# A two-layer graph network step: weight turns behind the first tiles, the takes spread over eight tiles, seven counting columns a pair, projection weights behind h1

## Chip, cores and metric

The kernel runs on one core of one Trainium2 chip. The metric is the device time in microseconds (us), given as the median of the runs. "Tile" below is 512 rows of the node table.

## What is computed

The input is a table x of 50,000 rows by 256 in float32 and 75,000 edges (src, dst), sorted by dst. They include a self edge for every node. Two layers follow each other, each with a residual:

```
h = relu(layernorm(x));  x = x + L0(h, src, dst)
h = relu(layernorm(x));  x = x + L1(h, src, dst)

L0: h = h @ w1.T + b1
    h = relu((h - mean) * rsqrt(var + eps) * gamma + beta)   # mean, var over all nodes
    xw = (h @ w2.T + b2) @ w_gcn.T
    deg = segment_sum(ones, dst) with one self loop more per node;  dinv = rsqrt(deg)
    out = segment_sum(xw[src] * dinv[src] * dinv[dst], dst) + b_gcn
L1: q, k, v = h @ Wq + bq, h @ Wk + bk, h @ Wv + bv          # 8 heads of 32
    a = softmax over the edges with the same src of (q[src] . k[dst])
    out = segment_sum(a * v[dst], src) @ Wo + bo
```

## The kernel before, in words

The node table has 98 tiles. All five engines run programs of their own and meet at semaphores. The kernel is a row of parts that end one after another; the change touches the first two.

**Part A, the first pass** (to about 605 us). For every tile SP loads x (two buffers, a_x), DVE takes the row moments (L215, L219), ACT the standard deviation (L648), DVE reciprocal and shift (L226, L228), and ACT normalises into a_hn (L652). PE turns a_hn (L680, eight transposes), ACT copies the turn to a_ht (L642), PE multiplies by w1 (L702) into one PSUM tile a_h_ps, ACT adds the bias and copies to h1 (L634) and stores it (L627), and DVE takes the column statistics of h1 (L1024). An engine's program is a list of steps; in step s it works on tile s less a lag: PE turns tile s - 1 and multiplies tile s - 3, ACT copies the turn of tile s - 2 and h1 of tile s - 4, DVE counts h1 of tile s - 5. `over_pairs` writes PE's and DVE's steps out, but for the pairs of tiles inside a hardware loop; `over_tiles` does the same for SP and ACT with one loop. A tile on PE waits until ACT has copied the last product out of a_h_ps.

Ahead of its first step PE waits for all seven loads of weights, turns w1 and w_gcn into turn_ps (L731), mixes w2 with w_gcn (L736) and the bias b2 with w_gcn (L739). ACT copies the results (L614, L616, L617), then issues eight loads of w_out (L621), and only then takes its first step.

Beside its tiles DVE sorts the edges for later parts (`beside_tile`, once per tile outside the loops). Tile 1 has the first preparation of the edge words (`pack_words`), tile 3 the second (`close_words`) and then all takes (`take_all`). A *take* finds the 8 largest of 294 words in each half of every partition, copies them to `found` and strikes them out (L836, L840, L841). The number of takes depends on the data; `take_all` is a loop over it. The class work, `decode_words` and what follows, stands behind tiles `class_tile` = 4 to 15. From pair `hist_pair` = 8 on DVE makes one-hot rows (L758, L759) of `hist_most` = 6 columns of edges a pair, three behind each tile. PE adds them up in hist_ps (L672), and POOL scatters the same columns to a table (L591). 240 columns make 40 pairs. These pairs are the loop `hist_loop`.

**Part B, the second pass** (to about 1145 us). SP loads h1 back (L1149), ACT applies the batch norm (L1198), PE multiplies by w_mix (L1231), DVE adds b_mix (L1310), ACT scales and stores y and agg_out. Between its tiles DVE and PE sort the takes by source. At its start SP loads two tiles of h1, waits for the turned roots of the degrees, stores them, loads the slots (L1169), then the projection weights and biases of the second layer (seven DMAs, L1171 to L1173), and only then h1 of tile 2. DVE searches the largest exponent of these weights (`find_peak`, L1323) behind its fourth tile step.

## Time and profile before

| | |
|---|---|
| median of 3 runs | 3427.66 us (3424.08 to 3429.75) |
| the profiled execution's own time | 3436.49 us |
| its span | 3434.7 us |
| mean granted TensorE clock in it | 0.967 |
| busy, share of the span | PE 90%, PE weight loads 73%, DVE 82%, ACT 73%, POOL 57% |
| DMA | 861 MB moved, mean 251 GB/s |

The profile is of one execution. The slices divide the span in 40 equal parts of 85.9 us and give each engine's busy share in tenths. In the timeline a row is one instruction or several alike merged: start and duration in us, engine, line, operation, output and inputs, count, and in brackets how long the engine had been idle before and what ended that. PEld is the load of a stationary operand; float32 matmuls show as two records each. SPq and ACTq rows are the issuing of DMAs. Busy shares of windows are sums over records in that stretch. The granted clock is the share of 2.4 GHz that TensorE was given.

### The profile page before, as it was taken

The numbers are of one execution on the slowest core, as the hardware profiler recorded it, in microseconds if no ns is written. First come the engines' busy times: TensorE is split into PE (matmuls) and PEld (weight loads), VectorE is DVE, ScalarE is ACT, GpSimd is POOL, SyncE is SP. The second block draws the span as 40 slices with busy tenths as digits, with TensorE's granted clock in tenths as the row PEclk, the third lists the DMA queues.
The fourth block names the chain that finished last, engine by engine and source line by source line (L and its number), as shares of the span: only waits on it lengthen the run. The fifth ranks groups of instructions, "written<-read, shape, count | busy, mean of one in ns | idle before, by whom it ended". The sixth has DMA issues, their size and how long they took to land. (4 is left out here: it accounts for less than half of the span.)

```text
span 3434.7 us, 80752 instructions
## 1 busy us (share of the span) xinstructions
PE 3104.5 (90%) x20244; PEld 2498.7 (73%) x20244; DVE 2809.3 (82%) x7375; ACT 2502.0 (73%) x7074; POOL 1953.0 (57%) x1668
## 2 busy tenths in 40 slices
PE   2899999799998489999999999994999999999999
PEld 1455554577775278787888878883899999999998
DVE  6888887787886478888888888884888888888887
ACT  2688888699896567676777777762777777777776
POOL 1055554155554377777777777763555555555553
PEclk6899999999999699999999999996999999999999
DMA  2455555688886578888878888865677777777774
GB/s 76 147 204 203 203 202 182 233 300 309 301 306 234 206 271 297 305 296 293 304 293 303 296 305 293 302 257 182 230 249 258 258 254 250 254 254 257 254 248 157
DMA packets 335634, 861.27 MB, mean 251 GB/s; under 512 B 98484, under 2 KB 152923, under 8 KB 323019
## 3 DMA queue, kind: packets, MB, share of 16 engines
q1 hardware_dynamic: 238794, 677.69, 55.3%
q0 software_dynamic: 66256, 78.94, 7.7%
q10 hardware_dynamic: 30512, 103.83, 7.6%
q8 instruction: 27, 0.44, 0.1%
q14 instruction: 45, 0.36, 0.0%
HBM read 521.95 MB, written 416.52 MB: 273 GB/s over the span
## 5 line engine op out<-in xcount | busy, mean ns | idle before, releaser
L1848 PE MATMUL c_qkv_ps<-w_qkv_hi,c_ht_hi 128*128 128x256 f16 x2352 | 642.3, 273 | 0.0
L1848 PE MATMUL c_qkv_ps<-w_qkv_lo,c_ht_hi 128*128 128x256 f16 x2352 | 642.3, 273 | 0.0
L1848 PE MATMUL c_qkv_ps<-w_qkv_hi,c_ht_lo 128*128 128x256 f16 x2352 | 642.3, 273 | 0.0
L2281 ACT ACTIVATE e_mine<-e_mine,e_attention 128x32 f32<-128x32 f32 x2352 | 518.7, 308 | 42.3 <-issue 26.1
L2228 POOL DMA_INDIRECT e_kv<-kv_table,e_near x392 | 401.5, 1024 | 113.4 <-issue 102.7
L1718 POOL DMA_INDIRECT c_got<-y_table,c_near x392 | 395.1, 1008 | 108.7 <-issue 87.9
L591 POOL DMA_INDIRECT dst_slots<-dst_word,dst_goal x240 | 241.3, 1005 | 304.3 <-ACT a_hn L652 235.9
L2317 PE MATMUL e_out_ps<-w_out,e_mean_t 128*128 128x256 f32 x1568 | 392.8, 380 | 0.0
L2220 POOL TENSOR_TENSOR e_kv<-e_kv,e_part_of 128x1024 f32<-128x1024 f32 x98 | 187.0, 1908 | 350.8 <-DVE e_part_of L2550 350.8
L702 PE MATMUL a_h_ps<-a_ht,w_t 128*128 128x512 f32 x784 | 368.9, 614 | 17.8 <-ACT h L634 13.9
L1482 POOL DMA_INDIRECT src_slots<-staged_word,staged_goal x240 | 235.2, 980 | 254.5 <-DVE sort_lane_hot L1371 119.2
L1231 PE MATMUL mix_ps<-w_mix,hb 128*128 128x256 f32 x1568 | 358.0, 382 | 12.7 <-ACT hb L1198 9.8
L1231 PEld LDWEIGHTS mix_ps<-w_mix,hb 128*128 128x128 f32 x1568 | 297.2, 191 | 59.0 <-ACT hb L1198 12.6
L1711 POOL TENSOR_TENSOR c_x<-c_agg,c_x 128x1024 f32<-128x1024 f32 x98 | 231.4, 2361 | 161.3 <-ACT c_agg L1765 151.9
L2317 PEld LDWEIGHTS e_out_ps<-w_out,e_mean_t 128*128 128x128 f32 x1568 | 267.4, 191 | 44.0
L1835 PE MATMUL c_sum_ps<-c_got,c_sum_hot 128*128 128x256 f32 x784 | 217.2, 400 | 87.3 <-DVE c_agg L1957 58.5
L702 PEld LDWEIGHTS a_h_ps<-a_ht,w_t 128*128 128x128 f32 x784 | 144.8, 195 | 184.2 <-issue 184.1
L1776 ACT ACTIVATE c_hn<-c_x,c_shift,c_rstd 128x256 f32<-128x256 f32 x392 | 203.5, 590 | 95.7 <-DVE c_shift L1978 94.8
L1703 POOL TENSOR_TENSOR c_qk<-c_q,c_kv 128x1024 f32<-128x1024 f32 x98 | 232.0, 2367 | 34.9 <-DVE c_kv L1942 32.6
L1848 PEld LDWEIGHTS c_qkv_ps<-w_qkv_lo,c_ht_hi 128*128 128x128 f16 x2352 | 230.5, 98 | 27.1
L1848 PEld LDWEIGHTS c_qkv_ps<-w_qkv_hi,c_ht_lo 128*128 128x128 f16 x2352 | 230.5, 98 | 27.1
L2273 ACT ACTIVATE e_mean_t<-e_mean_ps 128x512 f32<-128x512 f32 x196 | 114.9, 586 | 184.9 <-PE e_mean_ps L2331 163.8
(433 smaller groups left out, 7781.8 us busy)
## 6 DMA issues: line engine op xcount, KB each, us to landing
kv_table<-c_kv SPq DMA_DIRECT2D x98, 1024.0 KB
h_table<-h ACTq DMA_DIRECT2D x98, 512.0 KB
h<-h_table SPq DMA_DIRECT2D x98, 512.0 KB
y_table<-y_out ACTq DMA_DIRECT2D x98, 512.0 KB
agg_table<-agg_out SPq DMA_DIRECT2D x98, 512.0 KB
c_agg<-agg_table SPq DMA_DIRECT2D x98, 512.0 KB
x_table<-c_x SPq DMA_DIRECT2D x98, 512.0 KB
q_table<-c_q SPq DMA_DIRECT2D x98, 512.0 KB
```

The costliest lines, as they stand in the source:

```text
L591: nc.gpsimd.indirect_dma_start(out=dst_slots, out_offset=bass.IndirectOffsetOnAxis(ap=dst_goal[:, k:k + 1], axis=0), in_=dst_word[:, k:k + ...
L702: last = nc.tensor.matmul(h1_ps[:, oc * TILE:(oc + 1) * TILE], w1_t[:, kc, oc * P:(oc + 1) * P], ht[u][:, kc, :], start=kc == 0, stop=kc = ...
L1231: last = nc.tensor.matmul(mix_ps[u][:, j * D:(j + 1) * D], hb[u][:, kc, j * P:(j + 1) * P], w_mix[:, kc, :], start=kc == 0, stop=kc == KC - 1)
L1482: nc.gpsimd.indirect_dma_start(out=src_slots, out_offset=bass.IndirectOffsetOnAxis(ap=staged_goal[h][:, k:k + 1], axis=0), in_=staged_word ...
L1703: nc.gpsimd.tensor_tensor(qk[u][:, :, :], qb[w][:, :, :], kv[w][:, :, 0, :], ALU.mult).then_inc(qk_ready, 1)
L1711: nc.gpsimd.tensor_tensor(x1[u][:, :, :], agg[w][:, :, :], xb[w][:, :, :], ALU.add).then_inc(x1_ready, 1)
L1718: nc.gpsimd.indirect_dma_start(out=got[w][:, j, :], out_offset=None, in_=y_table, in_offset=bass.IndirectOffsetOnAxis(ap=near[w][:, j:j + ...
L1835: last = nc.tensor.matmul(sum_ps[:, j * D:(j + 1) * D], sum_hot[w][:, row, :], got[w][:, row, :], start=True, stop=True)
L1848: last = nc.tensor.matmul(qkv_ps[n][:, j * D:(j + 1) * D], h[u][:, kc, j * P:(j + 1) * P], wt[:, kc, n * D:(n + 1) * D], start=m == 0, sto ...
L2228: nc.gpsimd.indirect_dma_start(out=kv[w][:, j, :], out_offset=None, in_=kv_table, in_offset=bass.IndirectOffsetOnAxis(ap=near[w][:, j:j + ...
L2281: last = nc.scalar.activation(of_head, of_head, ACT.Copy, scale=attention[u][:, j, h, 0:1])
L2317: last = nc.tensor.matmul(out_ps[:, j, :], mean_t[u][:, kc, row * P:(row + 1) * P], w_out[:, kc, :], start=False, stop=kc == KC - 1)
```

## The change

Four things are changed.

1. PE's and ACT's first steps stand ahead of the weights. PE turns w1 and w_gcn behind its transposes of tile 1 (into a_h_ps instead of turn_ps), mixes w2 behind those of tile 2 and b2 behind those of tile 4 (both into hist_ps). ACT copies the turned weights behind tile 1, the mixed ones behind tiles 4 and 5. The eight loads of w_out are issued by SP, behind the edges. The class sums in hist_ps wait for the last copy.
2. Two takes stand behind each of tiles 4 to 11 (`take_pair` = 2, `take_pairs` = 4; pairs 3 to 5 are a loop, `take_loop`). The data-dependent rest, at least one take, is a loop behind tile 12 (`take_rest`). `class_tile` is 12, so all class work comes eight tiles later.
3. `hist_pair` becomes 12, so the columns have fewer pairs: `hist_most` is 7, four columns in the first tile of a pair and three in the second, and the loop has 34 pairs. The scatters on POOL go with them.
4. In part B the seven loads of projection weights stand behind the load of h1 tile 5, and `find_peak` stands behind DVE's sixth tile step.

```diff
-        self.takes_beside = -(-self.wide // TAKEN)
-        self.most_extra = max(1, self.most_takes - self.takes_beside + 1)
-        self.class_tile = 4
+        self.take_pair = 2
+        self.take_pairs = 4
+        self.takes_beside = 4 * self.take_pairs
+        self.most_extra = max(1, self.most_takes - self.takes_beside)
+        self.class_tile = 2 * (self.take_pair + self.take_pairs)
...
+                take_loop = (3, plan.take_pair + plan.take_pairs)
...
-                    return k is not None or i - plan.hist_pair in hist_pairs
+                    return k == 1 or (k is None and i - plan.hist_pair in hist_pairs)
...
+                            rows_of_head = wo.rearrange("(d h) n -> h d n", h=H)
+                            for h in range(H):
+                                kc, first = divmod(h * DH, P)
+                                sp.dma_start(w_out[first:first + DH, kc, :], rows_of_head[h]).then_inc(out_loaded, 16)
...
+                    sp.wait_ge(out_loaded, 16 * H)
...
+                    def copy_weights():
+                        for b, w in enumerate((w1_t, wg_t)):
+                            act.wait_ge(weights_turned, b + 1)
+                            nc.scalar.activation(w[:, :, :].rearrange("p a b -> p (a b)"), h1_ps[:, b * TILE:(b + 1) * TILE], ACT.Copy).then_inc(weights_copied, 1)
+
+                    def copy_mix():
+                        act.wait_ge(mixed, 1)
+                        nc.scalar.activation(w_mix[:, :, :].rearrange("p a b -> p (a b)"), hist_ps[:, 0:TILE], ACT.Copy).then_inc(weights_copied, 1)
+
+                    def copy_mix_bias():
+                        act.wait_ge(mixed, 2)
+                        nc.scalar.activation(b_mix[:, :], hist_ps[:, 0:D], ACT.Copy).then_inc(weights_copied, 1)
 
...
+                            if isinstance(i, int) and i * 2 + u == 1:
+                                copy_weights()
+                            if isinstance(i, int) and i * 2 + u == 4:
+                                copy_mix()
+                            if isinstance(i, int) and i * 2 + u == 5:
+                                copy_mix_bias()
...
-                    act.wait_ge(out_loaded, 16 * H)
...
+                        if s == 2:
+                            turn_weights()
+                        if s == 3:
+                            mix_weights()
+                        if s == 5:
+                            mix_bias()
                         if s == plan.class_tile + 6:
+                            pe.wait_ge(weights_copied, 4)
...
+                    def turn_weights():
+                        pe.wait_ge(weights_loaded, 16 * 7)
+                        for b, w in enumerate((w1_n, wg_n)):
+                            for kc in range(KC):
+                                for oc in range(KC):
+                                    at = b * TILE + kc * D + oc * P
+                                    last = nc.tensor.transpose(h1_ps[:, at:at + P], w[:, oc, kc * P:(kc + 1) * P], ident[:, :])
+                            last.then_inc(weights_turned, 1)
+                        pe.wait_ge(weights_copied, 2)
+
+                    def mix_weights():
+                        for kc in range(KC):
+                            for jc in range(KC):
+                                last = nc.tensor.matmul(hist_ps[:, kc * D:(kc + 1) * D], w2_n[:, jc, kc * P:(kc + 1) * P],
+                                                        wg_t[:, jc, :], start=jc == 0, stop=jc == KC - 1)
+                        last.then_inc(mixed, 1)
+
+                    def mix_bias():
+                        pe.wait_ge(weights_copied, 3)
+                        for jc in range(KC):
+                            last = nc.tensor.matmul(hist_ps[:, 0:D], b2_c[:, jc:jc + 1].to_broadcast([P, P]), wg_t[:, jc, :],
+                                                    start=jc == 0, stop=jc == KC - 1)
+                        last.then_inc(mixed, 1)
+
                     pe.wait_ge(const_ready, const_of_ident)
...
-                    over_pairs(pe, plan, 3, step, (hist_loop,))
+                    over_pairs(pe, plan, 3, step, (take_loop, hist_loop))
...
-                        link(v.tensor_scalar(rounds_f[:, 3:4], rounds_f[:, 2:3], -float(plan.takes_beside - 1), 1.0, ALU.add, ALU.max))
+                        link(v.tensor_scalar(rounds_f[:, 3:4], rounds_f[:, 2:3], -float(plan.takes_beside), 1.0, ALU.add, ALU.max))
...
-                    def take_all():
+                    def take_rest():
                         dve.wait_ge(const_ready, const_all)
                         more = dve.value_load(rounds[0:1, 3:4], min_val=0, max_val=plan.most_extra - 1) + 1
-                        with dve.Fori(0, more + (plan.takes_beside - 1)) as n:
-                            take(n)
-                        hold(dve, replaced, more * 2 + (2 * plan.takes_beside))
+                        with dve.Fori(0, more) as n:
+                            take(n + plan.takes_beside)
+                        hold(dve, replaced, more * 2 + (2 * plan.takes_beside + 2))
...
-                            take_all()
+                        elif 0 <= tile - 2 * plan.take_pair < 2 * plan.take_pairs:
+                            for m in two:
+                                take(2 * (tile - 2 * plan.take_pair) + m)
                         elif at == 0:
+                            take_rest()
...
-                            if k is None:
+                            if k == 0:
+                                for m in two:
+                                    take(i * 4 + (u * 2 + m - 4 * plan.take_pair))
+                            elif k is None:
...
+                    def load_qkv():
+                        for i, (w, b) in enumerate(((wq, bq), (wk, bk), (wv, bv))):
+                            sp.dma_start(w_qkv[:, :, i * D:(i + 1) * D], w.rearrange("(c p) n -> p c n", p=P)).then_inc(qkv_loaded, 16)
+                            sp.dma_start(b_raw[:, i * D:(i + 1) * D], b.partition_broadcast(P)).then_inc(qkv_loaded, 16)
+                        sp.dma_start(b_out_n[:, :], bo.partition_broadcast(P)).then_inc(qkv_loaded, 16)
...
+                            if isinstance(i, int) and i * 2 + u == 5:
+                                load_qkv()
...
-                            if isinstance(b, int) and b == 0 and t == 3:
+                            if isinstance(b, int) and b == 0 and t == 5:
```

The left-out lines take the old forms away: the weight turns ahead of PE's steps, the copies and w_out loads ahead of ACT's, and the projection loads behind `slots` in part B.

How the instructions move, in program order. On DVE, from the end of `close_words` (the last row of the second preparation, `rounds`) before: the takes are one loop, and tile 4's moments come behind it.

```order
L840 ISA
L840 COPY found<-edge_best 128x8
L841 MATCH_REPLACE words<-edge_best,words 128x294
L840 ISA
L840 COPY found<-edge_best 128x8
L841 MATCH_REPLACE words<-edge_best,words 128x294
L846 ISA
L846 COMPARE_AND_BRANCH
L341 ISA
L215 BN_STATS a_stats<-a_x 128x6 x4
L219 BN_AGGR a_moments<-a_stats 128x2 x4
```

The same place on DVE in the change (its own line numbers), from the last row of `close_words` on:

```order
L856 CAST rounds<-rounds_f 128x4
L217 BN_STATS a_stats<-a_x 128x6 x4
L221 BN_AGGR a_moments<-a_stats 128x2 x4
L228 RECIPROCAL a_rstd<-a_std 128x4
L230 SCALAR_TENSOR_TENSOR a_shift<-a_moments,a_rstd 128x4
L866 MAX edge_best<-words 128x8 x2
L870 COPY found<-edge_best 128x8
L871 MATCH_REPLACE words<-edge_best,words 128x294
L870 COPY found<-edge_best 128x8
L871 MATCH_REPLACE words<-edge_best,words 128x294
L866 MAX edge_best<-words 128x8 x2
```

Tile 4's moments and shift now follow the preparation directly, and its two takes stand behind them, ahead of tile 5.

On ACT, before, from the last bias load on (w_t and wg_t are the turned weights, w_mix and b_mix the mixed ones):

```order
L610 DMA b_c<-in_L_gnn_b 128x2x1
L614 ACT_TABLE_LOAD
L614 ACTIVATE w_t<-a_turn_ps 128x512
L614 ACTIVATE wg_t<-a_turn_ps 128x512
L616 ACTIVATE w_mix<-a_turn_ps 128x512
L617 ACTIVATE b_mix<-a_turn_ps 128x256
L621 DMA w_out<-in_L_gnn_Wo 32x256 x8
L648 ACT_TABLE_LOAD
L648 ACTIVATE a_std<-a_moments,eps_col 128x4
L652 ACTIVATE a_hn<-a_x,a_shift,a_rstd 128x256 x4
L648 ACTIVATE a_std<-a_moments,eps_col 128x4
L652 ACTIVATE a_hn<-a_x,a_shift,a_rstd 128x256 x4
```

and in the change:

```order
L618 DMA b_c<-in_L_gnn_b 128x2x1
L659 ACT_TABLE_LOAD
L659 ACTIVATE a_std<-a_moments,eps_col 128x4
L663 ACTIVATE a_hn<-a_x,a_shift,a_rstd 128x256 x4
L659 ACTIVATE a_std<-a_moments,eps_col 128x4
L663 ACTIVATE a_hn<-a_x,a_shift,a_rstd 128x256 x4
L624 ACTIVATE w_t<-a_h_ps 128x512
L624 ACTIVATE wg_t<-a_h_ps 128x512
L653 ACTIVATE a_ht<-a_turn_ps 128x512 x2
L659 ACTIVATE a_std<-a_moments,eps_col 128x4
L663 ACTIVATE a_hn<-a_x,a_shift,a_rstd 128x256 x4
```

Tiles 0 and 1 are normalised ahead of the copies of the turned weights, one table load is gone, and no w_out load is left on ACT.

On SP at the start of part B, before, from the load of `slots` on:

```order
L1169 DMA slots<-dst_slots 128x392
L1171 DMA w_qkv<-in_L_gnn_Wq 128x2x256
L1172 DMA b_raw<-in_L_gnn_bq 128x256
L1171 DMA w_qkv<-in_L_gnn_Wk 128x2x256
L1172 DMA b_raw<-in_L_gnn_bk 128x256
L1171 DMA w_qkv<-in_L_gnn_Wv 128x2x256
L1172 DMA b_raw<-in_L_gnn_bv 128x256
L1173 DMA b_out_n<-in_L_gnn_bo 128x256
L1149 DMA h_0<-h_table 128x1024
L1149 DMA h_1<-h_table 128x1024
L1149 DMA h_0<-h_table 128x1024
```

and in the change:

```order
L1213 DMA slots<-dst_slots 128x392
L1191 DMA h_0<-h_table 128x1024
L1191 DMA h_1<-h_table 128x1024
L1191 DMA h_0<-h_table 128x1024
L1205 DMA agg_table<-agg_out 128x1024
L1191 DMA h_1<-h_table 128x1024
L1186 DMA w_qkv<-in_L_gnn_Wq 128x2x256
L1187 DMA b_raw<-in_L_gnn_bq 128x256
```

The h1 loads of tiles 2 to 5 and the first store of agg_out now stand ahead of the weights, and the store of agg_out of tile 1 behind them.

## Rows read from the trace of the kernel before

**Rows 1.** The page's 40 slices, PE's busy tenths.
```profile
PE   2899999799998489999999999994999999999999
```

**Rows 2.** Timeline, part A's start: start, duration, engine, line, what, idle before.
```profile
6.15 0.38 DVE L219 BATCH_NORM_AGGREGATE a_moments<-a_stats 128x2 f32<-128x6 f32 x4
...
11.61 1.11 PE L731 MATMUL a_turn_ps<-ident,w_n 128*128 128x128 f32 x4 [11.61 <-DMA b_c<-in_L_gnn_b]
...
24.43 1.28 ACT L648 ACT_TABLE_LOAD   x1 [2.88 <-issue]
...
26.06 0.18 DVE L226 RECIPROCAL a_rstd<-a_std 128x4 f32<-128x4 f32 x1 [19.53 <-ACT a_std L648]
```

**Rows 3.** Timeline, DVE: preparations of the words, two takes, tile 4.
```profile
29.06 0.77 DVE L782 CAST edges_f<-edges 128x1176 f32<-128x1176 int32 x1
...
42.15 0.46 DVE L801 TENSOR_SCALAR work_i<-work_i 128x588 int32<-128x588 int32 x1
...
51.42 0.83 DVE L836 MAX8 edge_best<-words 128x8 f32<-128x294 f32 x2 [1.39 <-issue]
...
53.17 0.82 DVE L836 MAX8 edge_best<-words 128x8 f32<-128x294 f32 x2
...
77.88 1.41 DVE L215 BATCH_NORM_STATS2 a_stats<-a_x 128x6 f32<-128x256 f32 x4 [0.22 <-DVE words L841]
```

**Rows 4.** Timeline, PE and its weight loads behind the takes.
```profile
82.60 1.97 PE L680 MATMUL a_turn_ps<-ident,a_hn 128*128 128x128 f32 x8 [30.48 <-ACT a_hn L652]
...
85.22 0.34 PEld L702 LDWEIGHTS a_h_ps<-a_ht,w_t 128*128 128x128 f32 x1 [0.52 <-issue]
...
86.07 0.34 PEld L702 LDWEIGHTS a_h_ps<-a_ht,w_t 128*128 128x128 f32 x1 [0.52 <-issue]
```

**Rows 5.** Timeline of the column loop, then its window (PE, PEld, DVE, ACT, POOL busy).
```profile
302.38 0.66 PE L672 MATMUL hist_ps<-hot_hi,hot_lo 128*128 128x392 f16 x3
...
303.95 0.32 DVE L758 TENSOR_SCALAR hot_hi<-lane,dst_key 128x392 f16<-128x392 f16 x1
...
303.99 3.67 PE L702 MATMUL a_h_ps<-a_ht,w_t 128*128 128x512 f32 x8
...
304.34 0.32 DVE L758 TENSOR_SCALAR hot_hi<-lane,dst_key 128x392 f16<-128x392 f16 x1
...
309.24 3.67 PE L702 MATMUL a_h_ps<-a_ht,w_t 128*128 128x512 f32 x8 [0.21 <-ACT h L634]
...
314.36 3.67 PE L702 MATMUL a_h_ps<-a_ht,w_t 128*128 128x512 f32 x8
...
300.00:400.00 100.00, 97.30 (x365) 51.27 (x364) 88.28 (x346) 86.68 (x174) 58.59 (x59) 1.00 0.57 200
```

**Rows 6.** Timeline, DVE, tile 8: its moments and the h1 statistics in it.
```profile
108.90 1.41 DVE L215 BATCH_NORM_STATS2 a_stats<-a_x 128x6 f32<-128x256 f32 x4
...
111.38 1.28 DVE L1024 BATCH_NORM_STATS2 bn_stats<-h 128x6 f32<-128x512 f32 x2
```

**Rows 7.** Timeline, DVE: the starts of tiles 5, 16 and 24.
```profile
83.53 1.40 DVE L215 BATCH_NORM_STATS2 a_stats<-a_x 128x6 f32<-128x256 f32 x4
...
161.84 1.41 DVE L215 BATCH_NORM_STATS2 a_stats<-a_x 128x6 f32<-128x256 f32 x4 [0.21 <-DVE uneven_cols L940]
...
203.00 1.39 DVE L215 BATCH_NORM_STATS2 a_stats<-a_x 128x6 f32<-128x256 f32 x4
```

**Rows 8.** Window of tile 7: busy, then granted clock, DMA share, GB/s.
```profile
105.40:113.60 8.20, 4.76 (x16) 2.29 (x16) 7.70 (x26) 4.49 (x10) 0.00 (x0) 0.94 0.40 145
```

**Rows 9.** Timeline, part B's start (SP's queue and PE), then a window behind it.
```profile
623.43 9.41 SPq L1149 DMA_DIRECT2D h<-h_table  x3
...
624.79 3.62 PE L1231 MATMUL mix_ps<-w_mix,hb 128*128 128x256 f32 x16
...
632.54 3.72 PE L1231 MATMUL mix_ps<-w_mix,hb 128*128 128x256 f32 x16 [2.39 <-ACT hb L1198]
...
640.00:644.00 4.00, 2.86 (x16) 1.78 (x15) 3.83 (x18) 3.70 (x9) 0.00 (x0) 1.00 0.95 360
```

More of the change, by code:

```diff
@@ L733, in _ @@
-                    pe.wait_ge(weights_copied, 2)
-                    for kc in range(KC):
-                        for jc in range(KC):
-                            nc.tensor.matmul(turn_ps[1][:, kc * D:(kc + 1) * D], w2_n[:, jc, kc * P:(kc + 1) * P],
-                                             wg_t[:, jc, :], start=jc == 0, stop=jc == KC - 1)
-                    for jc in range(KC):
-                        last = nc.tensor.matmul(turn_ps[1][:, TILE:TILE + D], b2_c[:, jc:jc + 1].to_broadcast([P, P]), wg_t[:, jc, :],
-                                                start=jc == 0, stop=jc == KC - 1)
```

25 lines of the change are left out of this document (1 added, 24 removed).

## The prediction

> **What bounds the kernel now.** I read the slices of the page first, since they show where the matrix engine (PE) is not full. In the part that the change touches most, layer one's first pass (the first 605 of 3435 us), PE is full except in the first slice [rows 1]. Then I read the timeline there, engine by engine. The vector engine (DVE) has tile 0's moments at 6.5 us and then stands still for 19.53 us: the standard deviation that comes next waits on ACT behind the weight copies, eight DMA issues and a second table load, and the copies wait for weights that land at 11.6 [rows 2]. Later it is the other way round: DVE runs the takes alone, from 51.4 to 77.7, and PE is idle for 30.48 us [rows 3, 4]. In the steady stretch a pair of tiles takes 314.36 - 303.99 = 10.37 us, with PE 97%, DVE 88% and ACT 87% busy [rows 5]: nearly a balance, in which PE's products and the h1 copy on ACT set the pace. So what is saved before tile 24 is still saved at the end of the pass, if that balance holds. The chain that ended last lies in a later part and does not help here.
>
> **Step 1, the first tiles go ahead of the weights.** Tile 0's moments are ready at 6.5. ACT then needs its one table load, 1.28 us [rows 2]; standard deviation, reciprocal and shift follow, so tile 1 begins on DVE at about 8.6 and the first preparation of the edge words at about 11.5. From that preparation to the second it is 42.15 - 29.06 = 13.1 us, two tiles' moments among them [rows 3]. The second then starts at 11.5 + 13.1 = 24.6 instead of 42.15: **17.5 us** gained. The weight turns fit in between, since PE gets to them at about 14, after 11.6. The edges were issued ahead of the weights' last column and should be there at 11.5; if they land 2 us late, everything moves by 2. The eight w_out DMAs cost ACT 2.88 us of issue ahead of its table load [rows 2]; on SP they stand between the edges and tile 2's load, which waits until tile 0 is normalised at about 10.7 anyway. Without that cover they would cost 2.9.
>
> **Step 2, the takes.** A take is 53.17 - 51.42 = 1.75 us, and fifteen of them with their entry fill 50.0 to 77.9 [rows 3]. That block goes. The second preparation lasts 50.0 - 42.15 = 7.9, so tile 4 begins at 32.5, and tiles 4 to 11 carry two takes each. A tile without extra work costs DVE 111.38 - 108.90 + 1.28 = 3.76 us [rows 6], so a take tile is 3.76 + 3.49 = 7.25; eight are 58.0, less 1.3 because tile 4 has no h1 statistics. The cover for PE here is DVE: a tile's PE work is 8 x 0.85 + 1.97 = 8.8 us at the lower clock [rows 4], and at the higher a whole tile takes 5.1 to 5.3 [rows 5]. I add 1.5 for tile 4, where the first product, behind the mixing of the weights, may keep ACT from its standard deviation (0 to 3.4, half a product at the lower clock), and 1.5 for entering and leaving the new loop. No row shows such an entry alone; the nearest is the 1.39, with a register load, ahead of the takes [rows 3], so 0 to 3. Tile 12 begins at 32.5 + 58.0 - 1.3 + 3.0 = 92.2.
>
> **Step 3, the rest of the takes.** Sixteen are done by then and one more always runs, so there are two more than before. Tile 12 is old tile 4 (83.53 - 77.88 = 5.65 [rows 3, 7]) plus 1.3 of h1 statistics plus 1.39 + 1.75 + 0.2 for the last take: 10.3, to 102.5. Tiles 13 to 23 do what 5 to 15 did, 161.84 - 83.53 = 78.3 us, so tile 24 begins at 180.8. In the trace it begins at 203.0 [rows 7]. Steps 1 to 3 give **22.2 us**: 17.5 from the start and only 4.7 from the takes, because a take tile is 2 us longer than a steady one and two takes are added.
>
> **Step 4, seven columns a pair.** The 240 columns move from 40 pairs to 34. A tile's fourth column costs DVE 0.39 and PE at most 0.66 / 3 = 0.22 [rows 5]. The totals do not change; what counts is the slack in that tile. PE waits 0.21 for the h1 copy in one tile of each pair and not visibly in the other. So the price lies between 0 and 34 x 0.22 = 7.5 us. I take 1, since the tile without a visible wait still cannot start its product before the copy it needs. POOL goes from 58.6% busy [rows 5] to about 68%, and nobody waits for it before the pass ends.
>
> **Step 5, the projection weights.** At the start of the second pass SP issues 7 DMAs (1.28 MB) and only then, at 623.43, h1 tile 2; PE ends tile 1's product at 628.4 and starts tile 2's at 632.54 [rows 9]. With h1 first, the tile is there before PE wants it, and with its sort columns in between PE starts at about 629.4: 3.1 gained. The loads now fall behind tile 5's, where the 16 DMA engines are 0.95 busy [rows 9]; 1.28 MB at the 360 GB/s of that row is 3.6 us, half of which I count as given back by later tiles. The peak search that waits for them moves two tiles down with them. Net **1.3 us**, between a loss of 2 and a gain of 4.
>
> The Trainium skill (DMA: Bandwidth & Descriptors, on issuing engines) says that DMAs started by the scalar, sync or gpsimd engine all run on the same 16 engines and interleave. By that rule w_out saves no transfer time on SP and the projection loads only change place: step 5 would be 0 and the sum 1.3 less. No row here separates the two.
>
> **Sum.** 22.2 - 1.0 + 1.3 = 22.5 us. Against the profiled execution's own 3436.5 that is 3414.0. It stands 8.8 above the median of the three timed runs, 3427.7, and the saving is the same there: **3405.2**.
>
> **Rivals.**
> *The clock stays low in the take tiles.* For it: PE comes out of idle at the lower level, where a tile costs 8.8 us [rows 4]. Against it: from 105.4 to 113.6, with PE busy 4.8 of 8.2 us, the granted clock was 0.94 [rows 8]. At 1.2 GHz in all eight tiles PE would set 8.8 instead of 7.25: 12.4 lost, gain 10, 3417.6. The Trainium skill (TensorE: Matmul & The Clock Gate, Part 1) says that the throttled state is the default and activity releases it; by that rule 8.8 us of work in 7.25 could not stay throttled, and this rival would fall away. The trace agrees in that one window.
> *The balance breaks in the column pairs.* DVE's 0.39 and PE's 0.22 both land on the path: 0.61 x 34 = 21, gain 2.6, 3425. For it: 97% and 88% busy. Against it: both engines have some slack per pair, and all other tiles keep three columns.
> *Slower: the takes are not covered at all.* If something in the pipeline (the single h1 bank, or the h1 statistics that ACT waits for) makes a tile's matrix work and its takes run one after another, a take tile costs 8.8 + 3.5 = 12.3 us. Eight are 98.4, 40.4 more than I count: 22.5 becomes a loss of 17.9, 3445.6. It decides from a take tile of 7.25 + 22.5 / 8 = 10.1 us. Against it: DVE issues the shift and the h1 statistics ahead of the takes, so PE and ACT hold all that they need.
> *Nothing gained at the start:* something that I do not see, such as late edges, holds tile 0 or 1 back; the takes' 4.7 remain, 3422.7.
>
> **How the numbers follow.** My forecast with its inner bounds (tile 4, loop entry, columns, loads) has 0.82 and spans 3396 to 3415. The low clock has 0.07, the broken balance 0.03, nothing at the start 0.05, the slower case 0.03. The range is **3396 to 3416**: the forecast and a part-time low clock, about 0.15 left out. About 0.2% (6.9 us) is what a measurement of this kernel tells from no change. Faster by more: the forecast, the low clock and part of the others, 0.93; within: 0.04; slower: 0.03.
>
> **What would show it.** DVE: first reciprocal at about 8.3 and no idle of 19 us; second preparation at 24 to 26; take tiles 7.1 to 7.6 apart; tile 12's moments near 92 and tile 24's near 181. PE: no empty stretch of 30 us; pairs of 10.4 to 10.5 in the column loop. Second pass: tile 2's product within 1.5 us of tile 1's end. Wrong would be: take tiles above 8, pairs of 10.9, edges landing past 14 us, or a later product of the second pass held by h1's DMA for more than 3 us.

## The result, and the profile after

The changed kernel takes 3450.6 us (median of 20 runs) against 3427.6: a ratio of 1.0061, 95% interval 1.0039 to 1.0083. It is slower by 0.6%. The forecast was 22.5 us less, 3405.2 us, with a range of 3396 to 3416. Its runs scatter from 3422.1 to 3474.5 us, those of the kernel before only from 3424.1 to 3432.5. The profiled execution took 3447.9 us, near its median; that of the kernel before lay 8.8 us above its own.

The page of the changed kernel: the 40 slices, PE's busy tenths and its granted clock.

```profile
PE   6788998799998489999999999994999999999999
...
PEclk9999999899999779999999999996999999999999
```

The first slice went from 2 to 6 [rows 1], but slices 3, 4 and 7 fell from nine to eight and slice 2 from eight to seven. The start, in the timeline of the changed kernel:

```profile
5.87 0.38 DVE L221 BATCH_NORM_AGGREGATE a_moments<-a_stats 128x2 f32<-128x6 f32 x4
...
6.32 1.28 ACT L659 ACT_TABLE_LOAD   x1 [6.32 <-DVE a_moments L221]
...
7.95 0.18 DVE L228 RECIPROCAL a_rstd<-a_std 128x4 f32<-128x4 f32 x1 [1.70 <-ACT a_std L659]
...
10.95 0.77 DVE L812 CAST edges_f<-edges 128x1176 f32<-128x1176 int32 x1
...
24.08 0.46 DVE L831 TENSOR_SCALAR work_i<-work_i 128x588 int32<-128x588 int32 x1
...
32.23 1.40 DVE L217 BATCH_NORM_STATS2 a_stats<-a_x 128x6 f32<-128x256 f32 x4 [0.25 <-DVE rounds L856]
...
38.20 1.39 DVE L217 BATCH_NORM_STATS2 a_stats<-a_x 128x6 f32<-128x256 f32 x4
...
90.71 1.39 DVE L217 BATCH_NORM_STATS2 a_stats<-a_x 128x6 f32<-128x256 f32 x4
...
99.52 1.41 DVE L217 BATCH_NORM_STATS2 a_stats<-a_x 128x6 f32<-128x256 f32 x4
...
176.52 1.41 DVE L217 BATCH_NORM_STATS2 a_stats<-a_x 128x6 f32<-128x256 f32 x4 [0.22 <-DVE uneven_cols L970]
```

DVE's idle time of 19.53 us [rows 2] is 1.70. Tiles 4, 5, 12, 13 and 24 begin in the last five rows; tile 24 stood at 203.00 [rows 7], so 26.5 us are gained where the column loop begins, more than the 22.2 of the forecast. At the start of the second pass all of it is gone. Its first products after the change, timeline of PE:

```profile
647.04 3.62 PE L1271 MATMUL mix_ps<-w_mix,hb 128*128 128x256 f32 x16
...
652.24 3.62 PE L1271 MATMUL mix_ps<-w_mix,hb 128*128 128x256 f32 x16
```

Tile 1's product stood at 624.79 [rows 9] and is at 647.04: 22.2 us later. So the column loop lost 26.5 + 22.2 = 48.7 us. Two windows of the changed kernel, the one of [rows 8] and the one of [rows 5] (busy of PE, PEld, DVE, ACT, POOL, then granted clock, DMA share, GB/s):

```profile
105.40:113.60 8.20, 5.37 (x8) 2.01 (x8) 7.66 (x25) 2.92 (x7) 0.00 (x0) 0.79 0.27 98
300.00:400.00 100.00, 87.57 (x326) 46.27 (x325) 79.61 (x315) 74.50 (x150) 57.13 (x59) 0.97 0.52 174
```

In the first window, tile 13's and behind the rest of the takes, the granted clock is now 0.79 instead of 0.94. In the loop, the second window, PE fell from 97.3 to 87.6, DVE from 88.3 to 79.6 and ACT from 86.7 to 74.5 [rows 5]: no engine is the bound any more. What they wait for shows in one of six such places, timeline of the changed kernel:

```profile
236.24 3.67 PE L725 MATMUL a_h_ps<-a_ht,w_t 128*128 128x512 f32 x8
...
239.22 0.97 POOL L599 DMA_INDIRECT dst_slots<-dst_word,dst_goal  x1 [1.02 <-DMA dst_slots<-dst_word,dst_goal]
...
240.69 0.97 POOL L599 DMA_INDIRECT dst_slots<-dst_word,dst_goal  x1 [0.49 <-issue]
241.97 1.08 POOL L599 DMA_INDIRECT dst_slots<-dst_word,dst_goal  x1 [0.31 <-issue]
243.35 0.97 POOL L599 DMA_INDIRECT dst_slots<-dst_word,dst_goal  x1 [0.30 <-issue]
244.63 0.97 POOL L599 DMA_INDIRECT dst_slots<-dst_word,dst_goal  x1 [0.30 <-issue]
245.91 0.97 POOL L599 DMA_INDIRECT dst_slots<-dst_word,dst_goal  x1 [0.30 <-issue]
246.64 1.27 ACT L645 ACTIVATE h<-a_h_ps,bn_in 128x512 f32<-128x512 f32 x2 [6.72 <-remote]
...
248.05 4.57 PE L725 MATMUL a_h_ps<-a_ht,w_t 128*128 128x512 f32 x5 [6.77 <-ACT h L645]
```

PE's product ends at 239.91 by its record. The h1 copy on ACT starts at 246.64, and PE then waits for the copy. The copy waits for three semaphores: the product's, that of the store which frees its buffer (its last update stands in the trace at 235.53) and that of the statistics that DVE takes from the buffer (that instruction ended at 239.25). So the product's came last. "Remote" is what the view says when it finds no instruction of the core that ended just before the release; here the release is the product's own semaphore update, which the trace has at 246.48, 6.6 us after the last matmul. In the kernel before 111 of PE's 137 updates that its trace has from 200 to 480 us stand within 0.1 us of theirs. PE went on to the next transposes, which end at 241.28, and DVE to its one-hot rows, until 242.8; from then on only POOL works. The Trainium skill (Perfetto Trace Analysis, Per-engine timelines, on the Tensor Engine's instruction) says that the end of a matmul is the profiler's estimate. No run here can show whether the product was written late or only its semaphore passed on late; this text calls both a late update. The groups of waits from 200 to 600 us, changed kernel (engine, line, waited for: us in total, times, longest):

```profile
POOL dst_slots L599 <- issue: 74.6, 194, 2.8
POOL dst_slots L599 <- ACT a_hn L663: 71.6, 22, 10.2
...
ACT h L645 <- remote: 29.1, 6, 6.9
```

The kernel before has no wait of the kind "remote" in this stretch. It is not free of late updates, though. The other 26 of the 137, one in nearly every pair, come 1.3 to 2.9 us after the transposes, beside the row of six scatters, and no instruction in the profile has to wait for them: the delay is there, but covered.

The 29.1 us of waits are not the whole loss. Behind a stall PE works at the lower clock: the granted clock was 1.00 from 236 to 240 us and 0.50 from 248 to 252. From 203 to 605 us it was 1.00 before and is 0.96 after the change. As an estimate, 0.04 of these 402 us is at most 16 us; with the waits that is up to 45 of the 48.7.

### The profile page after: what moved, and what is told of

Its sections match the earlier page's. It is cut to its first block and busy times, and to the rows that moved or that the text cites. A ratio compares the mean times of both kernels' runs of the same rounds, so it can differ in the third digit from the quotient of the medians.

```text
span 3446.1 us, 80626 instructions
## 1 busy us (share of the span) xinstructions
PE 3119.8 (91%) x20244; PEld 2506.0 (73%) x20244; DVE 2814.0 (82%) x7391; ACT 2504.3 (73%) x7073; POOL 1953.3 (57%) x1668
## 5 line engine op out<-in xcount | busy, mean ns | idle before, releaser
L725 PE MATMUL a_h_ps<-a_ht,w_t 128*128 128x512 f32 x784 | 379.4, 629 | 51.3 <-ACT h L645 43.3
L1888 PEld LDWEIGHTS c_qkv_ps<-w_qkv_hi,c_ht_hi 128*128 128x128 f16 x2352 | 230.5, 98 | 24.7
```

The costliest lines, as they stand in the source:

```text
L725: last = nc.tensor.matmul(h1_ps[:, oc * TILE:(oc + 1) * TILE], w1_t[:, kc, oc * P:(oc + 1) * P], ht[u][:, kc, :], start=kc == 0, stop=kc = ...
L1888: last = nc.tensor.matmul(qkv_ps[n][:, j * D:(j + 1) * D], h[u][:, kc, j * P:(j + 1) * P], wt[:, kc, n * D:(n + 1) * D], start=m == 0, sto ...
```

## The experiments

The theories: **seven a pair** (the column loop loses by the seventh column or its scatter), against **early start** (it loses because it is entered earlier, or through two loops). Once that was settled, the theories became narrower.

One remark on the runs: step 5 alone and the first runs of the rows of twelve, of the even pauses and of six, six, seven ran beside a kernel before that took 3388 us, not 3427, and are compared with that alone. By the record these four, and no others, ran on chip 13; all other runs of this section ran on the chips 7, 11 and 12, where the kernel before took 3426 to 3427 us. For the runs of the result it names no chip.

### Seven columns alone, the early start alone

```
-        self.hist_most = -(-self.wide // (self.tiles // 2 - 1 - self.hist_pair))
+        self.hist_most = 7
```

> The kernel before with seven counting columns and seven scatters a pair (four beside one tile, three beside the next) and nothing else of the change; start and takes as before. Theory 'seven a pair' (the stalls of some 7 us in the column loop come with the seventh column or its scatter): the same stalls appear here, tile distances of 10 to 12 us at five or six places and a colder TensorE behind them; the column loop of the change lost some 47 us between tiles 24 and 97, so 3427.6 + 30 to 50 = 3458 to 3478 us, and the times scatter by tens of us. Rival 'early start' (the loop loses time because it is entered earlier, in another phase against the DMAs, or through two loops): nothing here, 3424 to 3432 us, tile distances of 5.12 and 5.26 us.

Measured: 3498.2 us (3477.2 to 3511.1), ratio 1.0222 [1.02, 1.0244]. Its waits from 180 to 570 us:

```profile
ACT h L634 <- remote: 33.0, 9, 5.2
```

The same stalls, with the start and the takes of the kernel before: 71.5 us lost against the 3426.7 beside it, more than the 30 to 50 that were expected. The other kernel is the changed one with these undone, and the projection weights' place too:

```
-        self.take_pair = 2
-        self.take_pairs = 4
-        self.takes_beside = 4 * self.take_pairs
-        self.most_extra = max(1, self.most_takes - self.takes_beside)
-        self.class_tile = 2 * (self.take_pair + self.take_pairs)
+        self.takes_beside = -(-self.wide // TAKEN)
+        self.most_extra = max(1, self.most_takes - self.takes_beside + 1)
+        self.class_tile = 4
...
                         elif at == 0:
-                            take_rest()
+                            take_all()
...
```

> The kernel before with the early start alone: weight turns behind the first tiles, output weights on SyncE's queue; the block of 26 us of takes at tile 4, six columns a pair and the projection weights as before. Theory 'seven a pair': no stalls, the start's 17.5 to 20 us stay until the end, 3407 to 3410 us, times within some 8 us of each other. Rival 'early start': stalls of 7 us in the loop again, 3430 to 3460 us and scattered.

Measured: 3406.7 us (3405.3 to 3408.7), ratio 0.9947 [0.9933, 0.996], so 20 us less than the 3426.7 beside it (14 to 23 by the interval), and no "remote" wait in the loop. The early start is innocent and gives what step 1 said, within the noise of this measurement.

### Column or scatter?

```
-        self.hist_most = -(-self.wide // (self.tiles // 2 - 1 - self.hist_pair))
-        self.hist_full = self.wide // self.hist_most
+        self.hist_most = 6
+        self.hist_full = 216 // self.hist_most
...
-                    for k in range(WIDTH):
-                        pair, c = divmod(k, per_pair)
+                    for k in range(216):
+                        pair, c = divmod(k, 6)
...
```

> The changed kernel with six columns and six scatters a pair, three a tile. It has 36 pairs for them, so the last 24 of 240 columns are neither counted nor scattered (10 per cent of the one-hots, of the counting products and of the scatters are left out). Theory 'seven a pair': no stalls, tile distances 5.12 and 5.26 us, first tile of the loop at 176 us as in the change, so some 26 us under the kernel before: 3399 to 3404 us, hardly scattered. Rival 'early start': as the change, 3430 to 3460 us, scattered.

Measured: 3407.2 us (3403.8 to 3409.5), 0.9948 [0.9934, 0.9961]. Only the second half of that edit, the loop of scatters, so that PE and DVE keep seven columns:

> The changed kernel with its seven columns a pair for VectorE and TensorE, but GpSimd scatters only six a pair, three beside each tile; the last 24 scatters are left out. If the fourth scatter in a tile (four times 1.28 us are the whole tile of 5.12 us) makes the stalls: none are left, and only the seventh column's own work remains, 3399 to 3410 us. If the four one-hot pairs and counting products in one tile make them: as the change, 3430 to 3470 us, scattered, with TensorE's product ending 7 us late at some places.

Measured: 3401.7 us (3398.7 to 3406.1), 0.993 [0.9917, 0.9944]. A window of it, to be held against the one above:

```profile
300.00:400.00 100.00, 97.87 (x375) 52.19 (x375) 92.37 (x370) 86.39 (x174) 57.01 (x58) 1.00 0.58 204
```

PE is back at 97.9%, and DVE at 92.4 carries the seventh column without a loss. (24 of 240 scatters are left out here; the last experiment below leaves none out and comes to 3407.3 us.) The converse, six columns with seven scatters (the first half of the edit, the loop of scatters left as it is):

> The changed kernel with seven scatters a pair (all 240), but six columns a pair for VectorE and TensorE; 216 of 240 columns are counted, the last 24 are left out. Theory 'scatters alone': the stalls are all there, 3430 to 3470 us, scattered. Rival 'both together' (the fourth scatter stalls TensorE only beside a fourth counting product): few or none, 3402 to 3412 us.

Measured: 3464.6 us (3439.4 to 3481.2), 1.0101 [1.007, 1.0132], with these waits:

```profile
ACT h L645 <- remote: 33.0, 7, 6.8
```

So the scatters alone make the stalls, and the columns' own work costs nothing that shows.

### How the scatters lie in time

```
-            ahead = 3
+            ahead = 2
```

> The changed kernel, seven columns and seven scatters a pair, but each scatter waits for the one two before it to land instead of the one three before it. Theory 'too many in flight' (the stalls need three scatters outstanding while the fourth is issued): with a landing some 2.0 to 2.2 us after the issue, two in flight still allow one scatter in 1.1 to 1.3 us, and no stall is left, 3400 to 3408 us. Rival 'row of scatters' (what counts is that they come one behind the other for a whole tile, 1.28 us apart): as the change, 3430 to 3470 us, scattered.

Measured: 3465.4 us (3463.1 to 3471.7), 1.0117 [1.0102, 1.0132]. By its time this is the rival's result, but the profile says otherwise: there is no "remote" wait, part A's last product is where it is without stalls, and the scatters go on until 642 us, 64 us after it. Timeline, POOL:

```profile
303.27 0.97 POOL L599 DMA_INDIRECT dst_slots<-dst_word,dst_goal  x1 [1.98 <-ACT a_hn L663]
304.55 0.99 POOL L599 DMA_INDIRECT dst_slots<-dst_word,dst_goal  x1 [0.30 <-issue]
307.75 0.97 POOL L599 DMA_INDIRECT dst_slots<-dst_word,dst_goal  x1 [2.21 <-DMA dst_slots<-dst_word,dst_goal]
```

POOL waits after every second or third scatter for a landing. With two in flight the stalls are gone, and a tail takes their place. No update of PE in the trace is more than 0.4 us late here, although seven scatters a pair were asked for: a pause of some 2 us after every two or three is enough.

```
-                    for k in range(WIDTH):
-                        pair, c = divmod(k, per_pair)
+                    for k in range(216):
+                        pair, c = divmod(k, 6)
...
-                        if c == per_tile:
-                            pool.wait_ge(hn_ready[1], pair + 1)
...
```

> The changed kernel with seven columns for VectorE and TensorE, and six scatters a pair as in the run with six scatters, but all six in a row beside the first tile of a pair and none beside the second; the last 24 scatters are left out. Theory 'length of a row' (four and more in a row make the stall): six in a row, 7.7 us of 10.4, stall at least as often as the change, 3430 to 3500 us. Rival 'rate' (seven scatters in 10.38 us are too many, six are not, however they lie): no stalls, 3399 to 3406 us.

Measured: 3408.7 us (3402.7 to 3410.6), 0.995 [0.9937, 0.9963]. It tells nothing new, since my picture of three beside each tile was wrong: the next pair's first wait, `hn_ready[0] >= pair`, asks for a tile that was normalised before the one this pair's second wait asks for. So POOL really stops once a pair: in the kernel before and in the run with six scatters six follow each other, in the change seven.

> The changed kernel with scatters that wait for no tile: from the first on they go one behind the other, three in flight, 1.28 us apart, so all 240 are done 307 us after the first instead of 380 to 410. Theory 'length of a row' or 'rate': stalls again and again while they run, the loop loses at least as much as in the change until some 480 us, nothing after: 3440 to 3520 us. Rival 'phase' (a stall needs a scatter that starts at one moment of the tile, which the wait for the normalised tile fixes): another number of stalls, possibly none, 3400 to 3425 us.

```
-                        if c == 0:
+                        if k == 0:
                             pool.wait_ge(hn_ready[0], pair)
-                        if c == per_tile:
-                            pool.wait_ge(hn_ready[1], pair + 1)
```

Measured: 3672.0 us (3670.1 to 3690.5), 1.073 [1.0709, 1.0751], far worse than any theory had it. Its windows (busy of PE, PEld, DVE, ACT, POOL, clock, DMA share, GB/s) and its longest waits from 230 to 500 us:

```profile
400.00:450.00 50.00, 2.09 (x13) 1.23 (x11) 1.67 (x9) 0.00 (x0) 37.44 (x40) 0.56 0.06 11
...
550.00:600.00 50.00, 48.92 (x185) 25.93 (x184) 45.74 (x183) 43.44 (x89) 0.00 (x0) 1.00 0.55 200
```

```profile
ACT h L643 <- remote: 155.0, 4, 51.2
PE a_h_ps L723 <- issue: 136.0, 3, 49.4
```

While POOL issues a scatter every 1.28 us, PE does 2 us of work in 50; a tile takes some 50 us. When the scatters are done (at 495 us) the loop runs as it should. The DMA engines are 6% busy meanwhile and move 11 GB/s, so this is no contention for transfers. From 200 to 480 us no update of DVE or ACT in this trace comes more than 0.02 us late; PE's are the ones that come late.

### Rate or length of a row?

> The changed kernel with scatters in rows of twelve: one wait every second pair, twelve in a row (15.4 us), then 5.4 us without any, so six in 10.38 us on average; the last 24 scatters are left out. It stands in for the earlier run with six at once, whose rows of six turned out to be those of the kernel before (its waits, too, let six follow each other). Theory 'length of a row' (seven in a row stall, six do not): stalls in each row, 3440 to 3520 us. Rival 'rate' (seven in 10.38 us are too many on average, six are not): none, 3399 to 3409 us.

```
-                        pair, c = divmod(k, per_pair)
-                        pair += plan.hist_pair
+                        pair, c = divmod(k, 12)
+                        pair = plan.hist_pair + 2 * pair
                         if c == 0:
-                            pool.wait_ge(hn_ready[0], pair)
-                        if c == per_tile:
                             pool.wait_ge(hn_ready[1], pair + 1)
...
```

Measured: 3364.8 us, 0.9929 [0.9916, 0.9943], beside 3388.

```
             ahead = 3
+            pause = sb("pause", [P, 170], where=part)
+            paused = sem("paused")
...
+                        if k > 0:
+                            if k > 1:
+                                pool.wait_ge(paused, k - 1)
+                            pool.memset(pause[:, :], 0.0).then_inc(paused, 1)
```

(and the tiles' waits left out, as in the free scatters)

> The changed kernel with all 240 scatters, none of which waits for a tile, but a fill of 170 numbers on GpSimd ahead of each, so that they come one by one some 1.45 to 1.6 us apart, as many in a pair of tiles as in the change, but evenly. Theory 'rate' (seven in 10.38 us): stalls as in the change or worse, 3430 to 3500 us. Rival 'row without a pause' (what holds TensorE's semaphores is that GpSimd goes from one scatter to the next without a pause): no stalls, 3400 to 3410 us, against 3672 us without the fills.

Measured: 3364.2 us, 0.9926 [0.9912, 0.9939], beside 3388; most scatters came 1.4 us apart.

```
-                    for k in range(WIDTH):
-                        pair, c = divmod(k, per_pair)
-                        pair += plan.hist_pair
+                    turn_of_column = [(pair, c) for pair in range(11, NT // 2) for c in range(7 if pair % 3 == 0 else 6)][:WIDTH]
...
+                    for k, (pair, c) in enumerate(turn_of_column):
...
```

> The changed kernel, nothing left out: VectorE and TensorE with seven columns a pair as in the change, scatters from tile 22 on in rows of six, six and seven over the 38 pairs that are left. Theory 'rate' with a threshold near seven, or 'length of a row' with stalls of which each costs some 7 us: at 6.3 in 10.38 us on average the rate theory has none (3400 to 3406 us); the row theory has some at its twelve rows of seven, at a third of the change's frequency (some 3415 to 3425 us, scattered).

Measured: 3364.2 us, 0.9927 [0.9914, 0.9941], beside 3388.

Three patterns and no stall in any. The even pauses alone would have spoken against the rate and the rows of twelve alone against the row, so neither theory fits all three; what fits is that nothing stalls on this chip. So the change itself and the free scatters ran again, beside two of the three.

> The change itself, nothing left out, as a control. Theory 'pattern of the scatters': its stalls are there on any chip, 0.3 to 1.3 per cent above the kernel before, scattered by tens of us. Rival 'another chip': no stalls, 0.7 per cent below the kernel before, as the last runs.

Measured: 3459.9 us (3441.0 to 3471.6), 1.0101 [1.0076, 1.0126], beside 3426.3.

> The scatters spread evenly by a fill of 170 numbers ahead of each, as before. If the pattern counts: 0.6 to 0.8 per cent below the kernel before beside a change that stalls. If rate alone counts and the last chip had no stalls: as slow as the change, 0.3 to 1.3 per cent above.

Measured: 3550.6 us (3531.6 to 3582.0), 1.0383 [1.0352, 1.0415]. Pauses of 0.4 us between all of them are worse than the change's rows of seven. Most scatters came 1.4 us apart and all 240 took 354 us, 1.48 us each, so some seven in 10.38 us, no more than in the change. At the same rate, pauses that are even but short cost more than rows with a longer one behind them.

> Rows of six, six and seven from tile 22 on, as before. Rate theory with a threshold above 6.3 in 10.38 us: 0.6 to 0.8 per cent below the kernel before, beside a change that stalls. Row theory: a third of the change's stalls, 0 to 0.4 per cent below, scattered.

Measured: 3442.0 us (3424.2 to 3456.6), 1.0041 [1.0019, 1.0064]. Timeline, the row of seven that began at 293.08 ends here, and a row of six follows:

```profile
299.57 1.01 POOL L599 DMA_INDIRECT dst_slots<-dst_word,dst_goal  x1 [0.30 <-issue]
300.89 0.97 POOL L599 DMA_INDIRECT dst_slots<-dst_word,dst_goal  x1 [0.30 <-issue]
303.46 0.97 POOL L599 DMA_INDIRECT dst_slots<-dst_word,dst_goal  x1 [1.60 <-ACT a_hn L663]
...
310.22 1.04 POOL L599 DMA_INDIRECT dst_slots<-dst_word,dst_goal  x1 [0.40 <-DMA dst_slots<-dst_word,dst_goal]
312.14 1.26 ACT L645 ACTIVATE h<-a_h_ps,bn_in 128x512 f32<-128x512 f32 x2 [3.70 <-remote]
313.55 5.37 PE L725 MATMUL a_h_ps<-a_ht,w_t 128*128 128x512 f32 x8 [3.43 <-ACT h L645]
```

Behind a row of seven the pause is 1.60 us, behind a row of six 2.67. This execution has 7 "remote" waits (23.0 us) in 180 to 570 us, where a row of seven comes every third pair. No such wait was found in a kernel with rows of six alone, though all five of them whose traces were taken on these chips have the covered late updates of the kernel before.

> The scatters that wait for no tile and have no pauses, as before: some 7 per cent above the kernel before if the stalls are a matter of the pattern on any chip; at most 1 per cent above if the first chip alone had them.

Measured: 3676.3 us (3671.7 to 3678.2), 1.073 [1.0715, 1.0746]: the first result again.

> Rows of twelve scatters (15.4 us), then 5.4 us without any, as before; the last 24 scatters are left out. In the runs on one chip each row of seven of the pattern six, six, seven came with one stall of some 7 us behind it and no row of six did. Row theory: stalls at all eighteen rows, 5 to 14 us each, 2 to 7 per cent above the kernel before. Rate theory: none, 0.6 to 0.8 per cent below. Should the kernel before take some 3388 us beside it, as it did once, it tells nothing.

Measured: 3556.9 us (3547.4 to 3564.2), 1.0378 [1.0363, 1.0393], beside 3427.4. Its waits, 180 to 570 us, then one row of twelve in the timeline, begun at 361.92:

```profile
ACT h L643 <- remote: 82.9, 11, 7.8
```

```profile
361.92 0.97 POOL L597 DMA_INDIRECT dst_slots<-dst_word,dst_goal  x1 [14.15 <-ACT a_hn L661]
...
362.88 3.67 PE L723 MATMUL a_h_ps<-a_ht,w_t 128*128 128x512 f32 x8 [0.21 <-ACT h L643]
...
366.58 1.26 ACT L643 ACTIVATE h<-a_h_ps,bn_in 128x512 f32<-128x512 f32 x2 [0.18 <-PE a_h_ps L723]
...
368.00 3.67 PE L723 MATMUL a_h_ps<-a_ht,w_t 128*128 128x512 f32 x8
...
376.62 0.97 POOL L597 DMA_INDIRECT dst_slots<-dst_word,dst_goal  x1 [0.30 <-issue]
379.35 1.26 ACT L643 ACTIVATE h<-a_h_ps,bn_in 128x512 f32<-128x512 f32 x2 [7.81 <-remote]
380.75 3.75 PE L723 MATMUL a_h_ps<-a_ht,w_t 128*128 128x512 f32 x4 [7.71 <-ACT h L643]
```

The average rate was meant to be that of the kernel before, six in 10.38 us; with the stalls the rows of twelve come some 30 us apart, so it is four. And it stalls at row after row. The product that ended at 366.55, 4.6 us into the row, reached ACT at once; the one that ended at 371.67, 9.8 us into it, reached ACT at 379.35, after the last scatter of the row. So what counts is how long the scatters go on without a real pause, not their rate. The rate theory falls. How long the pause must be was not found: 0.4 us was too short, some 2 us after two or three scatters and 2.7 us after six were enough.

### Step 5 alone, and a kernel that leaves nothing out

```
                                 load_h1(i, u)
+                            if isinstance(i, int) and i * 2 + u == 5:
+                                load_qkv()
...
-                            if isinstance(b, int) and b == 0 and t == 3:
+                            if isinstance(b, int) and b == 0 and t == 5:
                                 find_peak()
```

> The kernel before with the projection weights loaded behind h1 of tile 5 and nothing else of the change. Prediction step 5: 1.3 us less, bounds 4 us less to 2 us more, so 3425 us against 3426.5, nothing that the measurement can tell. Rival 'it frees the whole start of part B' (all that stood between TensorE's first and second product of part B was this load): 4 to 8 us less, 3419 to 3423 us.

Measured: 3390.5 us against 3388.3, 1.0006 [0.9996, 1.0015], 11 runs: 1.4 us less to 5 more. The rival's 4 to 8 us are not there. Step 5's 1.3 us less lies at the edge of the interval: it is not shown, and not quite excluded.

> The changed kernel, nothing left out: seven columns for VectorE and TensorE, scatters in rows of six from tile 22 on, the last twelve without a pause behind those of the last pair. Row theory: no stall in the loop; the last row of fifteen begins with the last tile and ends some 19 us later, with the landing 21 us, against 20 us until part A is done in the run with six scatters: 3402 to 3412 us, the upper end if the row holds TensorE's last products. Rate theory: the same, nearer to 3402.

```
                     for k in range(WIDTH):
-                        pair, c = divmod(k, per_pair)
-                        pair += plan.hist_pair
-                        if c == 0:
+                        pair, c = divmod(k, 6)
+                        pair += plan.hist_pair - 1
+                        if c == 0 and pair < NT // 2:
                             pool.wait_ge(hn_ready[0], pair)
-                        if c == per_tile:
+                        if c == 3 and pair < NT // 2:
                             pool.wait_ge(hn_ready[1], pair + 1)
```

Measured: 3407.3 us (3404.5 to 3412.8), 0.9946 [0.9933, 0.996], faster than both kernels, with nothing left out: 43 us less than the change's 3450.6. The last scatters, timeline of POOL and SP:

```profile
582.54 0.97 POOL L599 DMA_INDIRECT dst_slots<-dst_word,dst_goal  x1 [0.31 <-issue]
587.03 0.81 SPq L1191 DMA_DIRECT2D h<-h_table  x2
```

In the run with six scatters the second pass loaded h at 582.74 us, here at 587.03: 4 us of the takes' gain go into the tail. So it ends where the early start alone ends (3406.7), and of the two that one is the simpler.

## Why the prediction was wrong, step by step

**Step 1 was right.** First reciprocal 7.95 (8.3 forecast), first preparation 10.95 (11.5), second 24.08 (24.6). That is 18.1 us ahead, 17.5 forecast, and alone it gave 20 us (14 to 23 by the interval).

**Step 2 was right.** Tiles 5 to 11 took (90.71 - 38.20) / 7 = 7.50 us each, 7.25 forecast. Tile 4 took 5.97 instead of 7.45: the 1.5 for a late first product was not needed. Tile 12 began at 90.71, forecast 92.2. The rival of the low clock did not happen in the take tiles: from 38.20 to 90.71 the granted clock was 0.94.

**Step 3 was right** but for a few us: tile 13 at 99.52 (102.5), tile 24 at 176.52 (180.8).

**Step 4 failed.** Its price for DVE and PE, 1 us, between 0 and 7.5, was sound: with seven columns and six scatters nothing is lost against six and six (0.993 against 0.9948). What failed is its last sentence: "POOL goes from 58.6% busy [rows 5] to about 68%, and nobody waits for it before the pass ends". It counted POOL's busy time, asked who waits for POOL's results, and put the seven scatters at nothing. Nobody waits for the results; but PE's semaphore updates come late while POOL goes on issuing, and that cost 48.7 us in the profiled execution. In the medians it is 49 us against the 3401.7 with six scatters, of which 24 are left out, and 43 us against the 3407.3 of the last experiment, which leaves none out. The share of 68% said nothing; the seventh scatter turned a row of six with 2.7 us behind it into a row of seven with mostly 1.5 to 1.8 us, and the delay, covered before, reached PE's path.

**Step 5 was too hopeful.** Tile 1's product now ends at 647.04 + 3.62 = 650.66 and tile 2's begins at 652.24, 1.6 us later instead of 4.1; 1.0 was forecast. But alone the step measures 1.4 us less to 5 more, so its 1.3 us are at best at the edge. The traces show where it is given back. Tile 6's product begins 24.7 us after tile 1's, before the change 29.4; tile 8's begins 41.9 after it, before 40.5. In between stands this wait, timeline of the changed kernel:

```profile
669.78 1.52 ACT L1238 ACTIVATE hb<-h,bn_shift,bn_scale 128x512 f32<-128x512 f32 x2 [4.28 <-DMA h<-h_table]
```

That h load was issued at 662.54, behind the seven moved loads. So more than half was given back, which the prediction itself had named as a sign of being wrong: h's DMA holds a later product for more than 3 us.

**The rivals.** The slower one, at 3445.6 us, had the sign and came within 5 us of the time, but by luck: its mechanism did not happen, and the take tiles took 7.50 us, not 12.3. The broken balance had the right place (the column pairs) and about half the price, by work on PE and DVE that in fact costs nothing. None asked what another row of DMA issues on POOL does to engines that do not depend on it; the chance of 0.03 for slower was too small for a change that makes one engine's pattern denser in a part where PE, DVE and ACT are over 85% busy.

## What to carry to other kernels

When a step adds indirect DMAs issued by GpSimd, look at how many come one behind the other and how long the pause behind them is, not only at the engine's busy share; here six in a row (7.7 us) with 2.7 us behind them cost nothing that shows, and rows of seven cost 43 to 49 us, 1.3 to 1.4%. Every run here had indirect DMAs as POOL's load; none put other work of the same length in their place, so whether it is the issuing or any busy POOL is not shown. A wait that the profile calls "remote" on an engine that waits for a local TensorE result is the sign of it, and a time that scatters by tens of us where the kernel before holds 0.3% is the first hint. Test parts of a change alone: the early start by itself kept 20 us that the whole change threw away. And compare with the kernel before on the same chip, since a chip may show none of it.

## What the runs showed of the hardware

- Beside rows of GpSimd's indirect DMAs TensorE's semaphore updates come late: one wait lasted 51 us, with the DMA engines 6% busy. What in the chip holds them was not found. TensorE's are not the only ones: in the second run of the rows of twelve 20 of the 213 updates of VectorE that its trace has from 200 to 480 us are over 0.1 us late, one by 3.7 us. None of ScalarE's in that stretch was over 0.02 us late in any run.
- It is not so everywhere: beside the kernel before of 3388 us rows of twelve and scatters 1.4 us apart had no such wait at all, and all updates of TensorE in these traces from 200 to 480 us came within 0.02 us. The same kernels beside 3427 us lost 3.8%. By the record all runs beside 3388 us were on chip 13 and those beside 3427 us on the chips 7, 11 and 12, so it goes with the chip; chip 13 was used for one set of runs only, so a passing condition of it is not excluded.
- The same sign stands in the kernel before in its third stretch, 1200 to 2300 us, where POOL, mostly with indirect loads, is 76% busy. Waits of the kernel before there:

```profile
ACT c_ht_hi L1742 <- remote: 49.6, 41, 1.8
```

This wait stands in the traces of all runs on the chips 7, 11 and 12 (30 to 41 times) and in none of the four on chip 13. Most of the difference between the two kernels before arises there. In the profiled executions the start of the stretch's first transposes and of its last ones lie 1112.6 us apart in the kernel before and 1079.6 us in the run e3, 33 us less, of 51 between the two spans. In the first pass, whose rows of six delay only covered updates, the two differ by 1.5 us. That the waits are the whole cause of the 33 us was not tested.
- TensorE's clock pays too: from 203 to 605 us its granted clock was 1.00 before and 0.96 after the change, and 0.50 from 248 to 252 us, behind the stall shown above.
